# One ScalarE operation sums a whole group of w_proj where four did, and the preparation's step lists are written anew

## The reference

```
def xattn(x, ctx, ...):                  # x: 16x256x512, ctx: 16x256x384
    q = LN(LN(x)) @ Wq + bq ; k = LN(ctx) @ Wk + bk ; v = LN(ctx) @ Wv + bv
    return softmax(q k^T * 512**-0.5) @ v @ Wo + bo

def bitlinear(x, w):                     # w_fc: 2048x512, w_proj: 512x2048
    scale = clip(mean(abs(w), axis=1), 1e-5)
    tern  = clip(round(w / scale), -1, 1)
    return x @ (tern * scale).T

x = x + xattn(LN(x), ctx)
h = bitlinear(LN(x), w_fc) + gate * (LN(x) @ v.T @ fast_b.T @ u.T)
x = x + bitlinear(relu(h)**2, w_proj)
```

## Time and profile before

| | |
|---|---|
| median of three runs | 828.8 us (828.24 to 829.31) |
| the profiled execution, device time | 828.39 us |
| its span, first to last instruction | 826.6 us |
| TensorE busy | 810.5 us, 98% |
| VectorE, ScalarE, GpSimd busy | 62%, 45%, 19% |
| granted TensorE clock, mean | 1.000 |

### The profile page before, as it was taken

The page is one execution under the profiler, slowest core; times in us unless marked ns, Lnnn a source line. Parts: engine busy times, 40 slices in busy tenths (PEclk is TensorE's granted clock), DMA queues, the critical chain, the costliest instruction groups (busy, mean ns, idle before and its releaser), DMA issues.

```text
span 826.6 us, 11140 instructions
## 1 busy us (share of the span) xinstructions
PE 810.5 (98%) x4185; PEld 676.5 (82%) x4185; DVE 514.1 (62%) x1051; ACT 374.5 (45%) x712; POOL 154.1 (19%) x175
## 2 busy tenths in 40 slices
PE   6999999999999999999999999999999999999997
PEld 4678788888888888888888888888888888888886
DVE  5998763676547664676547764586536764477434
ACT  5997463424533263424634254424634255423332
POOL 2250230025001240024100150023300250013001
PEclk9999999999999999999999999999999999999999
DMA  9752010101101011101101011101101010000001
GB/s 317 254 148 91 1 52 1 38 1 52 52 1 39 5 48 50 39 1 51 52 1 40 1 52 51 39 1 52 52 1 39 0 52 1 1 2 26 25 1 51
DMA packets 17485, 36.74 MB, mean 44 GB/s; under 512 B 4596, under 2 KB 4998, under 8 KB 17432
## 3 DMA queue, kind: packets, MB, share of 16 engines
q1 hardware_dynamic: 16868, 34.98, 12.3%
q10 hardware_dynamic: 564, 1.06, 0.3%
HBM read 27.64 MB, written 8.39 MB: 44 GB/s over the span
## 4 chain that ended last, share of the span: by engine, by line
PE 94%; DVE 2%; DMA 2%; SPq 1%; issue 0%; ACT 0%; DVEq 0%
PE H L1194 28%; PE O L1174 28%; PE G L1090 24%; PE G L1118 4%; PE H L1200 4%; DMA Wv_s<-in_L_xattn_Wv_dram 2%; PE H L1074 1%; PE H L1090 1%; PE G L1147 1%; PE H L1118 1%; PE O L1247 1%; PE H L1067 1%; PE O L1215 1%; SPq L461 0%; PE H L1059 0%
## 5 line engine op out<-in xcount | busy, mean ns | idle before, releaser
L1194 PE MATMUL H<-xnT,fcT 128*128 128x512 f32 x1024 | 257.3, 393 | 0.0
L1174 PE MATMUL O<-projT,qbuf 128*128 128x512 f32 x1000 | 250.9, 393 | 0.0
L1194 PEld LDWEIGHTS H<-xnT,fcT 128*128 128x128 f32 x1024 | 188.3, 188 | 36.8
L1174 PEld LDWEIGHTS O<-projT,qbuf 128*128 128x128 f32 x1000 | 184.7, 188 | 37.1 <-DVE qbuf L986 0.3
L718 ACT ACTIVATE qbuf<-rbuf 128x512 fp32r<-128x512 f32 x126 | 79.5, 631 | 125.4 <-PE O L1174 63.6
L986 DVE TENSOR_TENSOR qbuf<-rbuf,qbuf 128x512 fp32r<-128x512 f32 x126 | 94.0, 746 | 65.2 <-ACT qbuf L718 65.2
L982 DVE TENSOR_TENSOR rbuf<-rbuf 128x512 f32<-128x512 f32 x128 | 98.7, 771 | 52.2 <-ACT rbuf L710 51.1
L710 ACT ACTIVATE rbuf<-H,scf 128x512 f32<-128x512 f32 x128 | 87.3, 682 | 81.8 <-PE H L1200 81.6
L571 POOL TENSOR_TENSOR xrs<-xrs,mhalf 128x4 f32<-128x4 f32 x9 | 9.5, 1050 | 347.5 <-DVE xrs L966 347.5
L1090 PE MATMUL G<-n1T,M 128*128 128x512 f32 x276 | 64.2, 390 | 0.0
L1090 PE MATMUL G<-Wvo,tT 128*128 128x512 f32 x270 | 63.9, 389 | 0.2 <-DVE tT L886 0.2
(11 more groups left out here) (169 smaller groups left out, 991.4 us busy)
## 6 DMA issues: line engine op xcount, KB each, us to landing
xb<-in_x_dram SPq DMA_DIRECT2D x8, 1024.0 KB
ctxb<-in_ctx_dram SPq DMA_DIRECT2D x8, 768.0 KB
wring<-in_L_ffn_w_fc_dram SPq DMA_DIRECT2D x16, 256.0 KB, 6.4
wring<-in_L_ffn_w_proj_dram SPq DMA_DIRECT2D x16, 256.0 KB, 3.8
out_dram<-x2a SPq DMA_DIRECT2D x8, 512.0 KB, 2.6
out_dram<-x2b SPq DMA_DIRECT2D x6, 512.0 KB, 2.6
Wq_s<-in_L_xattn_Wq_dram SPq DMA_DIRECT2D x4, 256.0 KB, 4.2
x2a<-in_L_xattn_Wo_dram ACTq DMA_DIRECT2D x1, 1024.0 KB, 11.3
```

The lines of the kernel that those rows point to most:

```text
L1174: mm = pe.matmul(banks[f"O{t}"][:, :], qbuf[:, j % 2, h, t * P:(t + 1) * P], projT[:, j, :], start=(j == 0 and h == HI), stop=(j == NFF - ...
L1194: pe.matmul(banks[f"H{j % 2}"][:, :], fcT[:, k, j * P:(j + 1) * P], xnT[:, h, k, :], start=(k == 0 and h == HI), stop=False)
```

## The change

ScalarE gets a step `sum:g`, which takes the absolute sum of all four pieces of a w_proj group in one operation of 128x2048. It waits until the four pieces have landed, writes its unused absolute values over `nrm`, and leaves one sum for each partition, so GpSimd no longer adds partial sums (two operations less for each of four groups). `abs:16` to `abs:31` are gone from the list; `sum:4` to `sum:7` stand in their place. All five lists are written in a new order. Among that: `store:3` goes from ScalarE to VectorE and `wqT:1` from VectorE to ScalarE, the joined pieces are 6, 7, 9, 12, 13, 14, 22, 23 instead of 5, 7, 8, 9, 10, 13, 15, 16, 20, and new kinds `lean` and `sign` are defined but stand in no list.

```
-        psum4 = sb("proj_row_sums", [P, 4])
...
+        absrow = nrm[:, :, :].rearrange("p a d -> p (a d)").bitcast(BF16)
...
-                            plink(nc.gpsimd.tensor_tensor(psum4[:, 0:2], asum[:, j, 0:2], asum[:, j, 2:4], ALU.add))
-                            plink(nc.gpsimd.tensor_tensor(psum4[:, 2:3], psum4[:, 0:1], psum4[:, 1:2], ALU.add))
-                            plink(nc.gpsimd.tensor_scalar(sc, psum4[:, 2:3], 1.0 / HID, EPS, ALU.mult, ALU.max))
+                            plink(nc.gpsimd.tensor_scalar(sc, asum[:, j, 0:1], 1.0 / HID, EPS, ALU.mult, ALU.max))
...
+                    elif kind == "sum":
+
+                        for i in range(4):
+                            act.wait_ge(ring_in[(4 * j + i) % 8], 16 * (j // 2 + 1))
+                        act.wait_ge(abs_done, 4 * j)
+                        nc.scalar.activation(absrow, wring[:, j % 2, :, :].rearrange("p a d -> p (a d)"), ACT.Abs,
+                                             accum_out=asum[:, j, 0:1]).then_inc(abs_done, 4)
```

Of the lists the diff shows here one line of each side (TensorE's, around the scores and `pT` of the first group of tokens):

```
-        "t:1 t:2 turn:20 turn:21 ut:0 turn:22 s:0 s:1 s:2 pT:0 s:3 ut:1 turn:23 ut:2 turn:24 pT:1 ut:3 w:0 w:1 w:2 "
+        "t:1 t:2 turn:20 turn:21 ut:0 turn:22 s:0 s:1 s:2 ut:1 turn:23 pT:0 s:3 ut:2 turn:24 ut:3 pT:1 w:0 w:1 w:2 "
```

More of the change, by code:

```diff
@@ L168 @@
     "sp": (
[3 rows of a table removed]
[3 rows of a table added]
+        "next "
     ).split(),
     "pe": (
[5 rows of a table removed]
[5 rows of a table added]
         "B.up:0 B.up:1 B.up:2 "
@@ L181 @@
     "act": (
[8 rows of a table removed]
[7 rows of a table added]
     ).split(),
     "dve": (
[6 rows of a table removed]
[6 rows of a table added]
     ).split(),
     "pool": (
-        "scale:0 tb xs23 scale:1 cs23 scale:2 scale:3 scale:4 scale:5 residual:0 residual:1 scale:6 residual:2 "
-        "residual:3 scale:7 a:0 a:1 B.xs23 a:2 a:3 B.cs23 "
+        "scale:0 tb xs23 scale:1 cs23 scale:2 scale:3 scale:4 scale:5 residual:0 residual:1 residual:2 residual:3 "
+        "scale:6 scale:7 a:0 a:1 B.xs23 a:2 a:3 B.cs23 "
     ).split(),
@@ L206 @@
 DVE_STORES = [int(word[6:]) for word in PROLOGUE["dve"] if word.startswith("store:")]
-JOINED = [int(word[5:]) for word in PROLOGUE["dve"] if word.startswith("tern:")]
+JOINED = [int(word[5:]) for word in PROLOGUE["dve"] if word.startswith(("tern:", "lean:"))]
+SIGNED = [int(word[5:]) for word in PROLOGUE["dve"] if word.startswith("lean:")]
 def prologue_steps(engine):
@@ L353, in mk_xattn_ffn @@
         bq_in, bo_in = sem("bq_in"), sem("bo_in")
-        sides_made = sem("sides_made")
+        sides_made, signs_made = sem("sides_made"), sem("signs_made")
         sprow_made = sem("sprow_made")
@@ L760, in steps @@
                                              accum_out=asum[:, j // 4, j % 4:j % 4 + 1]).then_inc(abs_done, 1)
+                    elif kind == "sum":
[4 more added lines that the diff above has]
+                                             accum_out=asum[:, j, 0:1]).then_inc(abs_done, 4)
+                    elif kind == "sign":
+                        gr, i = j // 4, j % 4
+                        act.wait_ge(scales_made, gr + 1)
+                        act.wait_ge(tern_turned, j - 3)
+                        here = half[:, gr % 2, i:i + 1] if gr < 4 else half[:, gr % 2, 0:1]
+                        nc.scalar.activation(below[:, j % 4, :], wring[:, gr % 2, i, :], ACT.Sign, bias=here
+                                             ).then_inc(signs_made, 1)
                     elif kind == "vecs":
@@ L987, in steps @@
                                                 ALU.subtract).then_inc(sqlo_made, 1)
-                    elif kind in ("sides", "tern"):
+                    elif kind in ("sides", "tern", "lean"):
                         gr, i = j // 4, j % 4
@@ L994, in steps @@
                             dve.wait_ge(tern_turned, j - 3)
+                        if kind == "lean":
+                            dve.wait_ge(signs_made, SIGNED.index(j) + 1)
+                            nc.vector.scalar_tensor_tensor(out=above[:, j % 4, :], in0=w, scalar=half[:, gr % 2, row],
+                                                           in1=below[:, j % 4, :], op0=ALU.is_gt, op1=ALU.min
+                                                           ).then_inc(sides_made, 1)
+                            continue
                         if kind == "tern":
```

## The result

The changed kernel takes 831.3 us (median of eight runs, 830.04 to 832.48) beside 828.5 us for the kernel before on the same chip (eight runs, 828.24 to 829.31). The ratio is 1.0034, with a 95% interval of 1.0025 to 1.0043: slower by 2.7 us, where 829.0 was forecast. The interval lies wholly above 1.002, so the loss is real though small; the time lies 0.06 us past the top of the predicted range.

A forecast was written before the change was run, and what follows sets the result against it. TensorE, without a gap from `M:2` to the end of `t`, was taken as the bound. Terms −0.3 + 0.45 + 0.05 = +0.2 us gave 828.6 us profiled, 829.0 on the median's scale, eight-in-ten range 827.2 to 831.2.

The forecast's parts named there:

- the wide sum's wait: ScalarE's `sum:4` to `sum:7` each wait for four pieces at once; cost 0, at worst about 0.5 us.
- this rival: A wide sum waits for its pieces and holds stores behind it: +0.5 to +1.5 us; chance 0.03 for more.
- No gap between `M:2` and `t`: TensorE stays full from `M:2` to the end of `t`; a gap over 0.3 us would prove the forecast wrong.
- Wo late: Wo, issued later on ScalarE, stalls TensorE at `wvo:0`, 5.3 us if in full; chance 0.15 for over 1.7 us.
- the landing of Wv: With 512 KB less ahead of it, Wv lands at about 22.4 us instead of 23.8.
- the step to `M:2`: TensorE starts `M:2` at about 25.3 to 25.4 us instead of 25.57; term −0.3 us.
- the wide sum's duration: On ScalarE, an operation of 128x2048 takes 1.8 to 2.1 us.
- "behind": From `a:0` on nothing changes, `turn:31` going into TensorE's waiting behind `B.x:3`; term 0.
- the two prices for a group's saving: ScalarE time saved by a wide sum per group: at most 1.1 us, floor 0.5 us; none enters the sum.
- The order from the scores to `w:0`: `ut:1` and `turn:23` move ahead of `pT:0` on TensorE; term +0.05 us, bounds −0.4 and +0.5.
- The joined pieces: Six instead of eight joined among pieces 0 to 19, eight more small matmuls on TensorE before `t`; term +0.45 us.

The follow-up runs named there:

- the low-rank loads early: Changed kernel with SyncE issuing bo and the seven small low-rank transfers ahead of piece 16 instead of behind piece 20: 830.0 us, ratio 1.0021.
- the filler: Changed kernel with `turn:25` moved between `pT:1` and `w:0`, its eight matmuls issued three times over: 830.8 us, ratio 1.0037.
- the `pT` order undone: Changed kernel with TensorE's order from `s:2` to `w:0` as before the change and ScalarE's `ut:2` behind `pT:1`: 830.65 us, ratio 1.0030.
- the three repairs: Changed kernel with low-rank loads ahead of piece 16, Wo ahead of the first `nx`, and `turn:25` repeated ahead of `w:0`: 829.4 us, ratio 1.0014.
- Wo early: Changed kernel with ScalarE issuing the load of Wo right behind `tb`: 832.0 us, ratio 1.0042.
- narrow group 5: Changed kernel with `sum:5` replaced by four narrow sums, GpSimd adding that group's partial sums as before: 830.0 us, ratio 1.0019.
- the `pT` order in the kernel before: Kernel before with the changed kernel's TensorE order from `s:2` to `w:0` and ScalarE's `ut:2` ahead of `s:3`: 830.1 us, ratio 1.0017.
- both moves of the first group: Changed kernel with Wo issued right behind `tb` and `n2T:1` copied ahead of `sum:5`: 830.75 us, ratio 1.0027.

## Why the prediction was wrong

**The step that failed: the wide sum's wait.** I had put it at 0 since "`sum:4` and `sum:5` stand behind several stores and products, late enough for their loads". For `sum:4` that held. For `sum:5` it didn't: it waited 1.55 us for its last piece in the changed kernel, and 1.0 to 2.4 us in the other kernels that kept it behind the low-rank loads. Where it waits, `t:0` follows its start by a fixed time (5.58 or 5.59 us in the four profiles of the changed lists with `n2T:1` behind it, 5.21 in the two with `n2T:1` ahead). In the two with the changed lists and no wait of `sum:5` it is 5.94 and 5.95 us: there `t:0` waits for nothing but TensorE's own work. Two runs undo it from opposite sides. Narrow sums in its place, with the loads unchanged, gave back 1.2 us; earlier loads, with the wide sum unchanged, 1.1 us. Together they show that neither the wide operation nor the loads cost this alone: it is the wide operation's need for the last piece, in a place where the last piece is late. I had looked at where the sum stands on its engine, and not at when SyncE issues its pieces, though the place of the low-rank loads stood in the list; and I had kept the 1.5 us of this rival to `sum:6` and `sum:7`, which cost nothing.

**No gap between `M:2` and `t`.** This was the condition under which I said I'd be wrong, and it is what happened: waits of 0.75, 1.06 and 0.18 us. TensorE had been full there, but full is no measure of slack. The copy of `n2T:1` came at 53.75 in the changed kernel and at 51.93 with the low-rank loads early, where TensorE stood at the same place (`M:3` at 50.19 and 50.07) and had no wait for it. Of these 1.7 us TensorE waited 1.06, so about 0.6 us was the lead.

**Wo late.** I gave it 0.15 for a stall of over 1.66 us. I had put the issue at 25.8 at the soonest, behind the operations ahead of it in the list. It came at 23.64, ahead of three of them (`M:1` starts at 23.67, `wvT:0` at 24.13, `store:2` at 24.61). Wo landed 9.1 us later, at about 32.7, and TensorE stood 0.75 us for it in that profile. Where `wvo:0` had no wait it came 6.43 us after `M:2` in three profiles; 6.4 was forecast. Other profiles with the same place of Wo in the list show a wait of 0.34 or none. So the rival was real, and smaller than its full 5.3 us. But by itself it makes at most 0.35 us of the loss: without it the stretch from `M:2` to `t:0` took 31.35 and 31.10 us (the filler, the `pT` order undone), where the changed kernel took 31.45.

**Right were** the landing of Wv (22.4, as forecast), the step to `M:2` (25.50, forecast 25.3 to 25.4, though it differs by more than that between profiles), the wide sum's duration (1.91 to 1.97 us in the changed kernel, forecast 1.8 to 2.1) and "behind" (constant shift from `t:0` to the first up projection, 99.51 after 96.84). Of the two prices for a group's saving the floor was right: from start to start a narrow sum takes 0.61 us (48.25 to 48.86) and the wide one 1.91 (51.36 to 53.27), so a group saves 0.5 us of ScalarE. The order from the scores to `w:0` moved no time in the profile, 0.01 us where +0.05 was forecast, although the waits of 0.32 us for `pT:0` and 1.07 for `w:0` became 0.49 for `pT:1` and 1.50 for `w:0`. With the order undone in the changed kernel the same stretch took 19.70 us, 0.03 less.

**The joined pieces.** The changed kernel has the eight small matmuls more that the term of +0.45 us counts, ahead of `M:2`, and in turn `n1T:1` behind it (0.44 us), as the working for `M:2` had it. Whether that much time would come back with two more joined pieces is not settled. Two fewer in the kernel before lengthened the stretch by 0.20 us, within what profiles differ by, and the medians can't tell it from nothing.

**What stays open.** With the three repairs 1.2 us of the loss are left by the ratio, of which 0.64 have a name (`n1T:1` 0.44 and the wait of 0.2 for WvT). The kernel with the low-rank loads early is 1.7 us slower than before by the ratio; falls of the clock, told of below, are a likely part of that. Neither removing the new order around `pT` nor filling its wait lowered the ratio clearly (1.0030 and 1.0037, after 1.0034). The longer waits for piece 23 in their profiles don't hide a gain, since the stretch up to `t:0` was no longer than the changed kernel's. But with six and five runs the intervals reach 0.9 us to either side, more than the 0.2 to 0.6 us expected, so they can't rule a small cost out. No version here beat the kernel before.

## What to carry to other kernels

Merging n small operations on n separately loaded tiles into one saves fixed costs, but it moves the start of all the work to the arrival of the last tile, and holds everything behind it on its engine. Before giving such a merge a price, write down when the last tile's load is *issued*, what stands ahead of it on its queue (many small packets above all), and what stands behind the merged operation on its engine. Two waits of one engine ahead of the same late event aren't two prices: measure from that event. And an engine without a gap says nothing of how far ahead its helpers are: read from the timeline how long before its use each tile is ready.

## What the runs showed of the hardware

**The granted clock can fall at a short wait in an otherwise busy kernel.** TensorE's wait of 1.5 us for `w:0` (in most kernels 2 us behind one of 0.5 for `pT:1`) ended in some executions in about 3 us at a clock of 0.50, the 1.2 GHz level. The kernel with Wo early is one of them (columns as in the earlier trace rows), and `w:0` to `w:1` in its timeline:

```profile
72.00:74.00 2.00, 1.51 (x18) 1.29 (x17) 1.93 (x7) 1.19 (x4) 0.00 (x0) 1.00 0.00 0
74.00:76.00 2.00, 0.50 (x5) 0.29 (x3) 1.68 (x5) 1.54 (x4) 0.00 (x0) 0.94 0.27 12
76.00:78.00 2.00, 2.00 (x10) 2.00 (x11) 2.00 (x4) 2.00 (x4) 0.00 (x0) 0.50 0.75 255
78.00:80.00 2.00, 2.00 (x14) 2.00 (x14) 1.71 (x10) 1.00 (x2) 0.59 (x3) 0.71 0.36 138
```

```profile
75.93 2.90 PE L1111 MATMUL H<-pT,n1T 128*128 128x256 f32 x12 [1.50 <-DVE pT L904]
```

`w:0` takes 2.90 us there instead of 1.67. The falls cost 1.4 to 1.5 us: from the start of `w:0` to that of `w:2` are 4.37 to 4.44 us in the four profiles and 2.95 in the changed kernel's. They were seen in four profiles (Wo early, narrow group 5, the `pT` order in the kernel before, low-rank loads early), always behind a wait of 1.5 us at `w:0`; the changed kernel's own profile, with the same waits, kept 1.00, as did the two others with them. None of the profiles in which `w:0` waited 1.07 us or less shows it. How often it happens can be estimated from the mean clock of each run. A mean of 0.996 occurs in 11 of 59 runs of the kernels with the 1.5 us wait (two of them the changed kernel's) and in none of 128 runs of the others. With the low-rank loads early the four runs at 0.996 took 830.2 to 831.8 us and the four at 1.000 took 828.7 to 829.8. The changed kernel's two, 831.83 and 832.48, are among its three slowest. So the falls very likely add to its time. How much of the median they make is not known: a mean of 0.998 stands both with the profiles that have a fall and with two that have none (both moves of the first group, the `pT` order undone), and the kernel with the filler alone did not get faster.

**When the same load lands differs by over 1 us between kernels that load alike up to there.** In the five profiles with the changed kernel's lists up to Wo's landing, Wo was issued between 23.1 and 24.0 us and took 5.6 to 9.1 us to land. In the five built on the lists of before it was issued between 18.9 and 19.6 and took 8.7 to 11.3. The last piece of group 5 came 1.0 to 2.4 us late for its sum. A wait that rests on such a landing has to be read from several profiles before it is given a size.
